# Spilling the second key tile to memory before the queries and first keys are stacked, in the first and fourth attention

## What is computed

```python
x = x + L0_xattn(layernorm(x), ctx, ctx, ..., mask)
x = x + L0_ffn(layernorm(x), ...)          # router, one expert of 8, and a shared one
x = x + L1_xattn(...); x = x + L1_ffn(...)
x = x + L2_xattn(...); x = x + L2_ffn(...)
x = x + L3_xattn(layernorm(x), ctx, ctx, mask, ...)
x = x + L3_ffn(...)

# an attention of 16 heads of 16, for each batch
q, k, v = heads(x @ Wq.T), heads(ctx @ Wk.T), heads(ctx @ Wv.T)
p = softmax(where(mask, fill, q @ k.T * 0.25))
out = merge(p @ v) @ Wo.T
```

## Time and profile before

| | us |
|---|---|
| median of 3 runs | 2326.16 |
| lowest and highest run | 2322.23 and 2326.80 |
| the profiled execution | 2323.39 |
| its span in the profile | 2321.6 |
| TensorE busy | 2169.4 (93%) |
| VectorE busy | 1285.7 (55%) |
| ScalarE busy | 1074.0 (46%) |
| GpSimd busy | 448.3 (19%) |

### The profile page before, as it was taken

The page is one execution under the profiler, slowest core; times in us unless marked ns, Lnnn a source line. Parts: engine busy times, 40 slices in busy tenths (PEclk is TensorE's granted clock), DMA queues, the critical chain, the costliest instruction groups (busy, mean ns, idle before and its releaser), DMA issues.

```text
span 2321.6 us, 46633 instructions
## 1 busy us (share of the span) xinstructions
PE 2169.4 (93%) x16038; PEld 1759.9 (76%) x16038; DVE 1285.7 (55%) x3563; ACT 1074.0 (46%) x2929; POOL 448.3 (19%) x478
## 2 busy tenths in 40 slices
PE   7999989999988899999999999999959979988998
PEld 6888877777666667678888788888747758877888
DVE  6877873222244522556556556555542238778766
ACT  5878872222223122244444444444402237877863
POOL 3112201111153345100000000000014421121150
PEclk9999999999999799999999999999969989999999
DMA  8677746222265322110000000001232257767701
GB/s 211 184 193 181 183 116 276 79 86 91 71 178 166 128 66 68 41 46 8 19 27 16 12 14 13 12 8 48 95 113 62 64 143 185 188 175 178 179 19 33
DMA packets 154867, 230.65 MB, mean 99 GB/s; under 512 B 66608, under 2 KB 127488, under 8 KB 152336
## 3 DMA queue, kind: packets, MB, share of 16 engines
q1 hardware_dynamic: 142160, 196.07, 30.4%
q0 software_dynamic: 10656, 29.37, 4.1%
q10 hardware_dynamic: 1824, 2.23, 0.4%
HBM read 176.36 MB, written 51.25 MB: 98 GB/s over the span
## 4 chain that ended last, share of the span: by engine, by line
PE 77%; DVE 7%; DMA 5%; issue 4%; SPq 3%; ACT 2%; POOL 1%; ACTq 0%; DVEq 0%; POOLq 0%
PE bank L2012 9%; PE bank L1157 8%; PE bank L2045 6%; PE bank L1188 6%; PE bank L1043 6%; PE bank L1039 6%; PE bank L2077 5%; PE bank L1083 4%; PE bank L1142 4%; PE bank L1028 3%; PE bank L1135 3%; PE bank L2062 3%; SPq L1523 2%; DMA query_halves<-arena 2%; PE bank L2398 2%
## 5 line engine op out<-in xcount | busy, mean ns | idle before, releaser
L1157 PE MATMUL bank<-ident,arena 112*125 112x112 f32 x2352 | 376.0, 278 | 2.2 <-DVE arena L1395 0.3
L1157 PEld LDWEIGHTS bank<-ident,arena 112*125 112x125 f32 x2352 | 342.8, 191 | 32.2 <-ACT arena L1428 5.8
L1428 ACT ACTIVATE arena<-arena,mx 112x375 f32<-112x375 f32 x512 | 309.3, 605 | 108.6 <-DVE mx L1374 104.5
L1374 DVE CUSTOM_DVE_ANT_0 arena<-bank,maskf 112x375 f32<-112x375 f32 x512 | 272.8, 541 | 101.3 <-PE bank L1135 96.8
L1428 ACT ACTIVATE arena<-bank,mx 112x375 f32<-112x375 f32 x272 | 154.8, 573 | 183.0 <-DVE mx L1386 155.4
L2012 PE MATMUL bank<-arena 128*128 x532 | 231.7, 558 | 2.1 <-ACT arena L2138 2.1
L1135 PE MATMUL bank<-kS,qS 128*112 128x376 f32 x512 | 204.9, 401 | 28.6 <-DMA qS<-query_halves 13.9
L1395 DVE COPY arena<-bank 125x336 f32<-125x336 f32 x448 | 214.1, 501 | 17.3 <-PE bank L1157 17.3
L1188 PE MATMUL bank<-arena 125*32 125x112 f32 (+1 forms) x4608 | 202.6, 265 | 3.1 <-DVE arena L1395 2.9
L1188 PEld LDWEIGHTS bank<-arena 125*32 125x32 f32 (+1 forms) x4608 | 144.3, 118 | 49.8 <-issue 32.5
L1435 ACT ACTIVATE arena<-bank 125x336 f32<-125x336 f32 x336 | 148.3, 442 | 45.4 <-PE bank L1157 44.4
(11 more groups left out here) (266 smaller groups left out, 3699.2 us busy)
## 6 DMA issues: line engine op xcount, KB each, us to landing
kS<-key_halves SPq DMA_DIRECT2D x256, 188.0 KB, 3.9
key_halves<-arena SPq DMA_DIRECT2D x64, 376.0 KB, 4.9
arena<-in_ctxT SPq DMA_DIRECT2D x62, 376.0 KB, 4.9
arena<-in_f_out SPq DMA_DIRECT2D x21, 768.0 KB, 4.5
qS<-query_halves SPq DMA_DIRECT2D x252, 56.0 KB, 2.2
arena<-in_f_up SPq DMA_DIRECT2D x4, 2816.0 KB, 20.0
arena<-results SPq DMA_DIRECT2D x38, 224.0 KB, 5.6
query_halves<-arena SPq DMA_DIRECT2D x32, 224.0 KB, 5.3
```

Source lines behind the costliest of these rows:

```text
L1157: m = pe.transpose(bank[2 + g % 2][0:KT, k * S:(k + 1) * S], pr[:, g % t.NR, k * KT:(k + 1) * KT], ident[0:S, 0:S])
L1374: dve.tensor_tensor_reduce(sm[:, g % 2, :], bank[g % 2][0:S, 0:SK], maskf[:, :], -t.a["scale"], 3e38, ALU.add, ALU.min, mx[:, g % t.NR:g % ...
L1428: act.activation(pr[:, g % t.NR, :], src, ACT.Exp, bias=mx[:, g % t.NR:g % t.NR + 1], scale=-1.0, accum_out=row_sum(t, b)[:, h:h + 1]).the ...
```

## The change

In the last branch of `batch(b)`, the spill of the second key tile moves from behind the stacking of the first keys to ahead of the stacking of queries. It keeps its own two waits (the halves of the second key tile, and the stacking of second keys of the batch before), and now also stands behind the wait for the scores of batch b-2.

```diff
                 spill_keys(0)
                 if b >= 2:
                     sp.wait_ge(t.scores, t.h0 + (b - 1) * t.H)
+                spill_keys(1)
                 stack_queries()
                 stack_keys(0)
-                spill_keys(1)
                 stack_keys(1)
```

## The result

| | before | changed |
|---|---|---|
| median of 4 runs each, us | 2324.2 (2317.9 to 2326.8) | 2361.9 (2351.5 to 2369.6) |
| ratio, 95% interval | | 1.0163 [1.0117, 1.021] |
| profiled execution, us (span) | 2323.4 (2321.6) | 2358.9 (2357.1) |
| first attention, 14 periods, us | 282.4 | 302.0 |
| fourth attention, 14 periods, us | 286.1 | 299.7 |

The direction and the mechanism were as forecast. The size was not: +37.7 us between the medians, +35.5 between the profiled executions, where +22 was forecast. Applied to the median of 2326.2 from which the forecast started, the ratio gives 2364 us, just above the range of 2334 to 2362; the median itself, 2361.9, lies at its upper end.

The account below looks back on a forecast made before the run. TensorE bounds the kernel, but waiting for the second keys makes SyncE's chain 20.9 us a period: 585.2 against 568.5 us over 28 periods, +16.7, plus 5 for clock falls, +22 in sum, giving 2348 us, range 2334 to 2362.

Parts of the forecast that it names:

- K leads the chain: SyncE's first query issue stands 0.5 us behind K, VectorE's completion of the second key tile, in nearly all 28 batches.
- From first query issue to first score: Stretch from SyncE's first query-stacking issue until TensorE may start the batch: 10.3 us, issues and landing included.
- waited case: Batch 11 of the first attention before the change, whose first score waited for the landing: 10.2 us from first query issue.
- TensorE idle at the first score: TensorE's first score waits for a key landing in 20 or more of 28 batches, 30 to 45 us in total.
- Stacking of second keys right behind the first: On SyncE's queue the second key stacking follows the first within 0.1 us, without the landing wait (5.6 us in batch 11).
- SyncE waits at the context: SyncE, running ahead after the key stackings, waits at the context's issue; no size given.
- S-to-K of 10.1: Mean time from a batch's first TensorE score to the next batch's second key tile complete in SBUF: 10.1 us.
- I expect two falls, as now: TensorE's clock falls to about 1.2 GHz twice after idle times, as before the change: +5 us.
- the five shorter waits left no such stretch: Of TensorE's seven waits before the change, only the two longest (3.2 and 2.7 us) were followed by slow clock.
- much slower: Rival, chance 0.08: idle time in every batch brings TensorE's clock down each time, 48 us plus 17 from the chain, 2391 us.
- Faster: Rival, chance 0.07: waits on key stacking (12.8 us) and two slow-clock stretches (4.8 us) vanish, 2309 us.
- No change: Rival, chance 0.09: a calmer queue shortens first query issue to score to 9.6 us, 2323 to 2328 us.

Follow-up runs that it names:

- e4: Kernel before, order of DMAs kept, with only SyncE's wait for the second key tile added ahead of the query stacking: 2355.1 us, ratio 1.0119.
- e3: Kernel before, with the spill of second keys moved between the stacking of queries and that of first keys: 2304.9 us, ratio 0.9912.
- e12: Changed kernel plus 12 TensorE transposes before first scores (not in the fourth attention's even batches), GpSimd's context halving held back: 2355.6 us, ratio 1.0129.

## Why the prediction was right about the sign and short in size

- **K leads the chain: right.** In 27 of 28 batches the first query issue stands 0.47 or 0.48 us behind K (0.5 forecast). e4 showed that the wait alone costs 1.2%, and e3 that all but the wait is a gain.
- **From first query issue to first score: right, with a wrong reason.** 10.42 us on average in both attentions, forecast 10.3. The forecast went above its waited case because the second spill's packets run ahead of the queries; e4 has 10.39 without them. With the 0.49 on average from K to the issue this is 10.9 against 10.8, or 2.9 us over 28 batches.
- **TensorE idle at the first score: right.** 24 waits with 35.1 us in all; 20 or more with 30 to 45 were forecast.
- **Stacking of second keys right behind the first: right.** It is the one row of 4.65 us, x8.
- **SyncE waits at the context: right in the fourth attention only, without effect.** In the first the context's issue follows the stacking at once (253.88 to 253.93), and the queue's slack is spent at the next spill of queries, 50.7 us. In the fourth SyncE waits 10.5 us there in eight waits (1.5 in three before), most of it in this row:

```profile
SPq L913 <- PE bank L1056: 9.0, 6, 2.2
```

- **S-to-K of 10.1: right for an undisturbed batch, wrong as a mean.** It is 9.5 to 9.7 in odd and 10.6 in even batches, as before, wherever no clock fall and no stall lies between. Batches 2 and 14 stand outside this alternation, which is thus not there "throughout": 9.8 and 10.5 us in the first attention, 11.3 and, without its fall, 9.5 in the fourth. The mean is 10.58. The forecast's sum had no term for VectorE's stalls, though the trace of before had 2.8 us of them. The measured sum over 28 periods is 28 x (10.58 + 0.49 + 10.42) = 601.7 us, and the two stretches last 601.75.
- **"I expect two falls, as now": this is the step that failed.** There were six falls with 27.3 us at the lower level, not two. The step rested on "the five shorter waits left no such stretch": five waits, none above 1.85 us, taken to show that 1.6 us is harmless. In the changed kernel falls followed waits of 1.57, 1.78, 1.81 and 1.98 us in the first attention and 1.94 us in the fourth, and one began within a wait of 2.40, while waits of 1.65, 1.66, 1.86 and 1.91 had none. The last of these, with the stretch after it at full clock:

```profile
322.19 0.43 PE L1135 MATMUL bank<-kS,qS 128*112 128x376 f32 x1 [1.91 <-DMA kS<-key_halves]
...
322.20:329.00 6.80, 6.80 (x68) 6.52 (x68) 4.64 (x16) 5.13 (x15) 0.00 (x0) 1.00 0.48 107
```

So the length of such a wait did not decide alone, and what else did stays open; each brought a chance of a fall, and there were 24 of them instead of seven. The forecast's range did allow for one to four more falls, and four more came; its central sum did not.

The falls can be priced from the rows, as what S-to-K exceeds the undisturbed value in those batches. Batch 12 of the first attention, whose second keys are below, has 269.92 - 256.19 = 13.73 in place of 10.6.

```profile
269.32 0.60 DVE L1254 SCALAR_TENSOR_TENSOR arena<-bank,biasA,arena 128x375 fp32r<-128x375 f32 x1
```

In the same way batches 3, 6 and 8 have 11.23, 12.15 and 12.12 us in place of 9.66, 10.59 and 10.59. That is 7.8 us in the first attention; in the fourth, batches 14 (11.05 in place of 9.5) and 15 (12.39 in place of 9.53) give 4.4. Together 12.2 us, about 7 more than the 5 of the forecast. The stalls behind GpSimd add 2.9 and the chain from K to the score 2.9, and S-to-K without falls and stalls is 1.5 us shorter over 28 batches than 28 x 10.1. These 11.5 us are the gap between 33.3 and 21.7 in the stretches. This division is arithmetic on one trace. What the runs show beside it is that falls and stalls occur, that their number changes from kernel to kernel, and that in one attention without them (e12's fourth) the chain has nearly its forecast length. Outside the stretches the span grew by 2.2 us, which was not traced.

The rival *much slower* was wrong in its extreme, a fall in every batch (2391), and right in its direction. The Trainium skill ("TensorE: Matmul & The Clock Gate", HAM oscillation) describes that case; here six falls came after 24 waits, so the page's picture holds in part. *Faster* was wrong for this order and near in price for e3. *No change* needed 9.6 us from issue to score; the mean was 10.4.

## What to carry to other kernels

A DMA queue issued in order is as late as the operand its next issue waits for: place a spill where its data has just become ready, behind issues that are ready sooner (here between the stackings, 0.9% faster than before, against 1.6% slower with a wait of 3.5 us for the data ahead of the queries), or give it to a queue on which nothing urgent stands behind it. To cost such a move, close the circle of the one period (score to operand, operand to issue, issue to landing) and compare it with the engine's own period. Then price disturbances as a rate per wait, not from the longest wait that happened to do no harm.

## What the hardware did that was not expected

- **The clock fell after short idle times, but not each time.** Waits of 1.57, 1.78, 1.81, 1.94 and 1.98 us at the first score were followed by a granted clock of 0.50 for 3.4 or 6.8 us; waits of 1.65, 1.66, 1.86 and 1.91 us were not. The same kernel had 27.3 us of it in one profiled execution and 34.1 in another.
- **A VectorE instruction stood still until GpSimd's ended.** L1354 took 1.11 us at batch 5 of the changed kernel, instead of 0.35, and ended 0.15 us after L793. The Trainium skill ("SBUF — State Buffer", Who interferes with whom) says that the two share a port pair when VectorE runs in a two-port mode, which it says `tensor_scalar` can enter, and that whoever issues first holds the pair for its whole instruction while the other is blocked fully. The times agree. The order agrees where the starts lie apart: L1354 keeps its 0.35 us at batch 13 before, where it starts 0.10 us ahead (L793 takes 1.91 us there), and L793 its 1.79 where it does. That the ports are the cause, no run here tests.
- **Filling TensorE's wait did not always keep its clock.** e12 has 12 transposes ahead of each first score of the first attention (batches 2 to 15), and three falls there, after waits of 1.02 to 1.98 us that were left behind the transposes.
